# Identity transposes ahead of and behind the first rows' transposes in a graph layer with a mixture of experts

## The reference

```python
def _L0_gnn_ref(x, adjacency, node_degree, W, b):
    a_hat = adjacency + jnp.eye(n)
    dinv = jax.lax.rsqrt(node_degree)
    a_norm = dinv * a_hat * dinv          # node_degree is [n, 1]: both factors act on the row
    pooled = a_norm @ x + x
    return jax.nn.relu(pooled @ W + b)

def _L0_ffn_ref(x, gate_w, w1, w2, w3, sw1, sw2):
    logits = xf @ gate_w.T                # top 1 of 8 experts, its weight from a softmax
    h = silu(xf @ w1[e].T) * (xf @ w3[e].T)
    y = (h * comb) @ w2[e].T
    y = y + gelu(xf @ sw1.T) @ sw2.T      # the shared expert

deg = jnp.maximum((adj != 0).sum(-1), 1.0)
x = x + _L0_gnn_ref(_layernorm(x), adj, deg[..., None], L0_gnn_W, L0_gnn_b)
x = x + _L0_ffn_ref(_layernorm(x)[None], ...)[0]
```

## Time and profile before

| | |
|---|---|
| median of 3 executions | 483.42 us (483.39 to 485.46) |
| profiled execution | 486.0 us |
| its span | 484.4 us |
| busy share of the span: PE, POOL, DVE, ACT | 92%, 69%, 56%, 42% |
| mean granted clock of TensorE over the span | 0.989 of full speed |
| share of PE in the chain that ended last | 45% |
| share of POOL in that chain | 19% |

### The profile page before, as it was taken

How to read it: one execution, slowest core, us unless ns; L and a number is a source line. 1 busy time by engine, 2 the same in 40 slices (tenths; PEclk the granted TensorE clock), 3 DMA queues, 4 the chain that set the end, 5 groups by cost and what they waited for, 6 DMA issues and landing times.

```text
span 484.4 us, 8954 instructions
## 1 busy us (share of the span) xinstructions
PE 445.1 (92%) x2620; PEld 380.8 (79%) x2621; DVE 270.8 (56%) x549; ACT 203.3 (42%) x449; POOL 336.5 (69%) x309
## 2 busy tenths in 40 slices
PE   5899967999989999979988999999999999999992
PEld 5788845898869878868966888888888888888872
DVE  4998687654974498767773334233433333343330
ACT  3656458464545554574542233222323322232330
POOL 2888947276985799757796467976788579884112
PEclk9999999999999999999998999999999999999998
DMA  7565442201360055568676599997999563644000
GB/s 243 192 210 172 130 129 89 100 1 47 128 216 2 1 167 182 160 217 319 179 225 187 194 393 343 326 339 248 317 326 335 166 244 87 81 61 64 0 1 0
DMA packets 41004, 82.61 MB, mean 171 GB/s; under 512 B 5008, under 2 KB 16656, under 8 KB 38928
## 3 DMA queue, kind: packets, MB, share of 16 engines
q1 hardware_dynamic: 28416, 47.60, 30.1%
q0 software_dynamic: 7536, 29.39, 19.4%
q10 hardware_dynamic: 5024, 5.27, 3.7%
HBM read 74.74 MB, written 8.41 MB: 172 GB/s over the span
## 4 chain that ended last, share of the span: by engine, by line
PE 45%; POOL 19%; issue 9%; DMA 5%; DVE 3%; ACT 3%; SPq 2%; POOLq 1%; ACTq 0%
PE bank L1356 19%; POOL a_lo L447 10%; PE bank L1383 7%; POOL ering L493 5%; PE bank L1275 4%; PE bank L1297 4%; PE bank L1384 4%; DMA ering<-in_experts 3%; PE bank L1369 3%; POOL sorted_x L522 2%; PE bank L1299 2%; DMA eraw<-in_experts 2%; POOL gel_lo L463 2%; SPq L378 1%; ACT a_hi L605 1%
## 5 line engine op out<-in xcount | busy, mean ns | idle before, releaser
L1356 PE MATMUL bank<-ering,xsT_hi 128*128 x368 | 121.6, 402 | 1.9 <-POOL ering L493 1.8
L447 POOL TENSOR_TENSOR a_lo<-araw,a_hi 128x512 fp32r<-128x512 f32 x64 | 97.0, 1533 | 27.7 <-ACT a_hi L605 27.6
L1181 PE MATMUL bank<-zz,a_hi 128*128 128x512 f32 (+1 forms) x256 | 93.0, 402 | 9.8 <-POOL a_lo L447 9.6
L1100 DVE SCALAR_TENSOR_TENSOR hid<-bank,xs,sil 128x512 f32<-128x512 f32 x46 | 34.5, 751 | 92.5 <-ACT sil L740 90.5
L1356 PEld LDWEIGHTS bank<-ering,xsT_hi 128*128 128x128 f32 x368 | 69.9, 190 | 17.5 <-issue 2.7
L493 POOL TENSOR_TENSOR ering<-eraw,ering 128x512 fp32r<-128x512 f32 x40 | 51.9, 1317 | 29.7 <-DMA ering<-in_experts 20.1
L1356 PE MATMUL bank<-ering,xsT_lo 128*128 x184 | 72.4, 393 | 0.0
L1183 PE MATMUL bank<-zz,a_lo 128*128 128x256 f32 (+1 forms) x256 | 71.7, 280 | 0.0
L740 ACT ACTIVATE sil<-bank 128x512 f32<-128x512 f32 x46 | 27.5, 598 | 101.4 <-PE bank L1356 99.3
L1383 PE MATMUL bank<-ering,hidT_hi 128*128 x184 | 67.4, 406 | 1.2 <-DVE hidT_lo L1108 1.2
L1181 PEld LDWEIGHTS bank<-zz,a_hi 128*128 128x128 f32 x256 | 48.0, 188 | 24.2 <-issue 11.7
(11 more groups left out here) (156 smaller groups left out, 826.7 us busy)
## 6 DMA issues: line engine op xcount, KB each, us to landing
araw<-in_adj_t SPq DMA_DIRECT2D x32, 512.0 KB, 3.9
eraw<-in_experts SPq DMA_DIRECT2D x48, 256.0 KB, 5.0
ering<-in_experts POOLq DMA_DIRECT2D x8, 1536.0 KB, 9.0
eraw_more<-in_experts SPq DMA_DIRECT2D x48, 256.0 KB, 5.9
ering<-in_experts POOLq DMA_DIRECT2D x8, 1024.0 KB, 6.7
ering<-in_experts POOLq DMA_DIRECT2D x8, 512.0 KB, 4.8
xs<-sorted_x ACTq DMA_DIRECT2D x20, 129.0 KB, 4.7
resid<-in_x SPq DMA_DIRECT2D x4, 512.0 KB, 9.2
```

The lines of the kernel that those rows point to most:

```text
L447: pool.tensor_tensor(a_lo[:, u % AR, :], araw[:, u // CJ, u % CJ, :], a_hi[:, u % AR, :].bitcast(F32), ALU.subtract).then_inc(adj_lo_ok, 1)
L1181: pe.matmul(acc(q, it)[:, :], a_hi[:, s, it * P:(it + 1) * P], zt, start=first, stop=False)
L1356: ins = pe.matmul(bank[2 * w + h][:, :], a[:, k, :], ering[:, bass.ds(slot, 1), part, at:at + BANK].rearrange("p a n -> p (a n)"), start=n ...
```

## The change

TensorE waits for the identity alone instead of all four constants, runs 31 identity transposes there instead of 20, and five more between the transposes of the first tile and those of the second. The wait for the four constants moves to the first place at which TensorE reads `ones`.

```diff
-            pe.wait_ge(consts, 4)
-            keep_clock_up(20)
+            pe.wait_ge(consts, 1)
+            keep_clock_up(31)
             xn_transpose(0)
+            keep_clock_up(5)
             pe.wait_ge(split_lo, 1)
             for t in range(NT):
@@
                 pe.wait_ge(z_ok, t + 1)
                 agg_part(0, t, t % AR, t)
+            pe.wait_ge(consts, 4)
             degrees(0)
```

## The result

The changed kernel took 487.55 us (median of 22 executions, 485.17 to 491.59). The kernel before, run beside it, took 485.53 us (median of 22, 483.39 to 488.94); of its first three, from which the prediction started, two were the lowest of all 22. The ratio is 1.0048, with a 95% interval of 1.0028 to 1.0067: the change made the kernel slower by 2.0 us, where 0.5 us less was forecast. The profiled execution took 486.63 us, with a span of 485.1.

A forecast was written before the change was run, and what follows sets the result against it. TensorE was taken as busy nearly throughout, with a cold clock after 10 us the only reachable loss at the start. Terms 0 + 0 + 0 - 0.5 us from the median 483.42 gave 482.9 us, range 482.0 to 484.9.

The forecast's parts named there:

- What bounds the kernel: Whole kernel: TensorE busy nearly throughout; the change acts only through the first ten microseconds and the clock behind them.
- the earlier start: Kernel start: identity transposes begin at 1.78 us, the 31 end at about 7.8, before the first tile at 8.44; cost 0.
- the five: Behind the first tile: five transposes hidden by the wait for `w_lo`; cost 0 warm, at most 0.1 us cold.
- the moved wait: Before `degrees(0)`, end of the first quarter: the fourth constant is finished at 2.88 us, so cost 0.
- What keeps the clock up: 7.05 to 10.01 us: TensorE's work grows from 0.44 to about 1.9 us, so the clock stays at 2.4 GHz.
- What that gives: Tile 4's rows at 17.76 us: they come 0.5 us earlier, at least 0.28 and at most 0.83.
- moves by the same 0.5: VectorE behind ScalarE's second copy: `zz` at 14.38 us, then aggregates, count and normalized rows, all 0.5 us earlier.
- That split: ScalarE's split of the first adjacency block at 11.22 us: tied to the block landing at 11.24, it cannot move.
- There is no slack in which the 0.5 would vanish: 18 to 60 us: VectorE, then TensorE, is busy nearly throughout, so the 0.5 us gain reaches the end.
- A cold stretch in the experts, slower: Rival, 13 in 100: the fall at 262.53 to 265.94 us becomes usual, costing 1.7 us; time 484.6 us.
- The clock falls all the same: Rival, 17 in 100: the clock rises as early as 3.5 us and still falls at 10; nothing gained, 483.4 us.
- Transposes do not hold the clock: Rival, 2 in 100: no rise from the start's transposes, tiles one and two 0.2 us later and cold; 483.6 us.

The follow-up runs named there:

- g1_look: Changed kernel, no edit, one execution for its profile; no median, its 31 transposes took 5.69 us.
- g2_look: Changed kernel, no edit, one more execution for its profile; no median, its 31 transposes took 5.59 us.
- e2_no_five: Changed kernel without the five transposes behind the first tile: 486.22 us against 485.62 for the kernel before, ratio 1.0013.
- e3_five_only: Kernel before plus only the five transposes behind the first tile, old start and 20 ahead: 485.97 us against 485.62, ratio 1.0011.
- e4_gaps: Changed kernel plus 10, 7 and 7 identity transposes ahead of the waits for tiles 4, 8 and 12: 485.72 us against 485.62 before, ratio 1.0004.
- f2_gap8_12: Changed kernel plus seven identity transposes ahead of each wait for tiles 8 and 12, none for tile 4: 487.48 us against 486.30 before, ratio 1.0028.
- f1_gap4: Changed kernel plus ten identity transposes ahead of tile 4's wait alone: 485.97 us against 486.30 for the kernel before, ratio 0.9994.
- f4_quiet: e4_gaps plus six transposes ahead of second-quarter adjacency blocks 4 to 11 and twelve before the first repeated expert step: 486.11 us against 486.30 before, ratio 1.0011.
- e1_again: Changed kernel run again, no edit: 487.75 us against 485.62 for the kernel before, ratio 1.0041.

## Why the prediction was wrong

**What bounds the kernel, the earlier start, the five, the moved wait:** right. The first transpose began at 1.77 (1.78 forecast), the 31 ended at 8.12 (7.8), the five at 9.64 and the second tile's transposes still waited for `w_lo`. None of the three shows a cost; the 0.2 us by which the first tile came later in this profile is x landing later, and is absent in g1_look and g2_look, where it starts at 8.32 and 8.44.

**What keeps the clock up:** right for 10 us. In all nine profiles in the table the clock is 1.00 from 10.0 to 13.4 us.

**What that gives:** the direction was right and the size too large. ScalarE's second copy moved by 0.72 us in that profile, the rows that release tile 4 by 0.3 (0.5 forecast), tile 4 by 0.02 to 0.25 in the eight profiles with the early start and the five. The step that failed first is that VectorE's work behind the second product "moves by the same 0.5": the count (L833) took 1.23 us and not 0.76. I took its duration for fixed. In all 14 profiles it started anywhere from 14.27 to 15.11 us and took 0.66 to 1.31 us, but it ended 0.54 to 0.60 us behind the end of GpSimd's second subtraction. So its end follows GpSimd, whose work goes on without a pause from its first subtraction, behind ScalarE's first split and the landing of the first block. Starting the count earlier gains nothing. That split was said not to move, and began at 10.98 us, 0.24 earlier, as the block took 8.9 us to land and not 9.2; so part of the little that was gained in this profile is not the clock's. Why the count's end follows GpSimd's no run shows.

**"There is no slack in which the 0.5 would vanish":** this is the step that turned the sign. I used the missing slack for the gain and did not ask what a fall of the clock would cost in the same chain. The wait of 1.77 us ahead of tile 4 stood in the rows, longer than both idle stretches that I had just called the cause of the fall at 10. The sum has no term for a fall there: I took the wait as harmless because the clock had held in it, in one execution. It had held behind a cold stretch. With the clock up from 10 us on, TensorE is done with the work ahead of this wait at 15.5 instead of 16.0, the wait grows to 1.9 or 2.0 us, and in the profiles in which the clock rises late the fall comes here. The price is 1.4 us from tile 4 to tile 5, against 0.2 us for the fall at 10.

**The cause, as far as the runs show it:** the change moves a fall of the clock from a cheap place to a dear one. At 10 us the chain is held by a landing block and by ScalarE, and by GpSimd behind them; from 17.7 us on ScalarE's copy of each tile waits for TensorE (0.89 us in the row at 20.58, 1.85 in the row at 21.80 behind the cold stretch). Filling tile 4's wait alone takes the slowdown away, filling it together with the other two in the kernel before changes nothing that can be told, and leaving out either part of the padding at the start (e2_no_five, e3_five_only) takes most of the loss away.

**The rivals.** "A cold stretch in the experts, slower" (13 in 100) had the right kind of mechanism, a fall moved by a small displacement, at the wrong place. A fall at the experts is part of the loss in the first profile. The changed kernel's first profile and e4_gaps have the same start (6.35 and 6.37 us for the 31). Tile 5 is 1.42 us apart and the last tile 1.22; the two executions are 2.3 us apart (486.63 and 484.33). The rest is at the first expert step. Busy us by stretch, changed kernel:

```profile
262.00:267.00 5.00, 3.90 (x10) 3.11 (x11) 2.11 (x5) 0.40 (x1) 1.56 (x2) 0.66 0.65 199
```

and e4_gaps:

```profile
262.00:267.00 5.00, 4.85 (x21) 4.01 (x22) 2.25 (x6) 0.60 (x1) 0.81 (x1) 1.00 0.56 173
```

There the clock fell in the first and not in the second, which had a fall near 76 us instead, worth 0.5 us. One pair can't tell whether the change causes the fall at the experts, but the other profiles speak against it. Between 258 and 272 us the clock falls in both profiles of the kernel before and in four of the five of kernels with the fall at 10, and in four of the eight of the others whose transposes there are unchanged. So it is not what the change makes usual. The rivals "The clock falls all the same" and "Transposes do not hold the clock" are both out: in nine profiles the clock was 1.00 behind the padding, and ten transposes in tile 4's wait left it there.

**The numbers.** The forecast stood on a median of three, 483.42 us, which 22 executions put at 485.53. That alone moves the forecast to 485.0 and leaves its sign wrong. The range ended at 484.9 and was 0.3 us below the lowest execution of the changed kernel.

**What stays open.** In the profiles the dear fall came in two of five where the whole change stood with its wait open and started early (table), at 1.3 and 1.4 us. That alone makes some 0.5 us in the mean, not 2. The mean granted clock, which is on record for each timed execution, narrows this. Its median is 0.986 over the 22 executions of the changed kernel and 0.985 for f2_gap8_12, but 0.9885 for f1_gap4. A stretch of 3.4 us at the lower level takes 0.0035 off it (half of 3.4 us in 485). So, as an estimate, filling tile 4's wait spares about one whole stretch in the typical timed execution, more than the profiles show. For the kernel before the median of 35 is 0.987: the change leaves about as much cold time as there was, in dearer places. Whether those are all tile 4's wait, or a fall there also draws later ones after it as in the pair above, is not shown. Nor does the clock alone set the time: f4_quiet has 0.9905 against 0.986 for the kernel before beside it, and gained nothing.

No version tried beats the kernel before. The nearest, f1_gap4, has a ratio of 0.9994 (0.9971 to 1.0017).

## What to carry to other kernels

Where TensorE's clock can fall in several waits, keeping it up in one may only pass the fall to a later one. So before padding a wait, list all the later ones with their lengths, and price a cold stretch at each by what bounds the chain there: a wait that follows a cold stretch in the trace has not been shown to be safe. Fill the wait whose cold stretch is dearest, and judge by many executions, since the place of the falls changes from one to the next.

## What the runs showed of the hardware

The moment of the clock's first rise is not fixed: the same 31 transposes took 5.59 to 6.35 us in four profiles of the same kernel, and the one with 6.35 is the one in which the clock fell some ten microseconds later. A wait of 2.00 us left the clock at 1.00 in g2_look, while one of 1.92 us had it at 0.50 in the first profile of the same kernel, so the length of a wait alone does not say whether it falls.

The page's clock column reads 1.00 while the identity transposes still take the cold 417 ns: at the start the durations tell the clock, the column does not.

How long VectorE's count over 128x1024 elements takes depended on when it began beside GpSimd's subtraction: 1.31 us from 14.27 us on in e1_again, 0.66 us from 15.11 on in e3_five_only, with its end 0.55 and 0.60 us behind the subtraction's.

Three stretches at the lower clock, each of 3.4 us, cost very different amounts: 0.2 us of the end at 10 us, 1.4 at 17.7, and in the experts, where TensorE is busy throughout, the estimate of 1.7 from the earlier trace rows stands against about 1.5 between e4_gaps and the kernel before, from the first `sil` (254.63 and 254.27) to that of the third step (274.61 and 275.76).
